# A routing search of ten steps instead of eleven, and a token order made over eight periods instead of three

## The reference, cut to what matters

```python
x = L0_attn_x                      # 16 batches x 512 tokens x 256
xn = _layernorm(x, axis=-1)
x = x + attention(xn, Wq, Wk, Wv, Wo, qn_w, kn_w) + ffn(xn, centroids, ln_g, ln_b, w1, b1, w2, b2)

# attention: 16 heads of 16; q and k normalized per head (rms), softmax, Wo
# ffn: a mixture of 8 experts with balanced assignment
def balanced_assignment(scores):   # T = 8192 tokens, E = 8, C = T // E = 1024
    taken = jnp.zeros((T,), dtype=bool)
    for e in range(E):
        s = jnp.where(taken, -jnp.inf, scores[:, e])
        _, idx = jax.lax.top_k(s, C)
        parts.append(idx)
        taken = taken.at[idx].set(True)
    return jnp.concatenate(parts)
# routed = feat[order]; out = routed + w2(gelu(w1(layer_norm(routed)))); put back by the inverse order
```

## Time and profile before

| | us |
|---|---|
| median of three runs | 1078.44 |
| lowest and highest | 1077.86, 1079.5 |
| the profiled execution, its own time | 1079.18 |
| its span in the profile | 1077.4 |
| TensorE busy in it | 1038.7 (96%) |
| VectorE busy | 802.4 (74%) |
| ScalarE busy | 744.2 (69%) |
| GpSimd busy | 714.3 (66%) |

### The profile page before, as it was taken

The page is one execution under the profiler, slowest core; times in us unless marked ns, Lnnn a source line. Parts: engine busy times, 40 slices in busy tenths (PEclk is TensorE's granted clock), DMA queues, the critical chain, the costliest instruction groups (busy, mean ns, idle before and its releaser), DMA issues.

```text
span 1077.4 us, 20796 instructions
## 1 busy us (share of the span) xinstructions
PE 1038.7 (96%) x7222; PEld 673.6 (63%) x7222; DVE 802.4 (74%) x1893; ACT 744.2 (69%) x966; POOL 714.3 (66%) x753
## 2 busy tenths in 40 slices
PE   4899999999999999999999998999999999999997
PEld 3445555454544454545454443589888999988897
DVE  8899896777777768777767678786768767777861
ACT  3588888888888888888888886763555555355550
POOL 5677878676767767677687656646665676766434
PEclk9899999999999999999999999999999999999999
DMA  4544744443443543534534455133534334453313
GB/s 154 187 158 141 241 163 144 145 163 125 160 165 109 188 146 109 206 119 139 176 128 154 151 176 173 67 104 82 128 54 123 82 82 93 89 129 53 65 20 40
DMA packets 83531, 138.15 MB, mean 128 GB/s; under 512 B 9937, under 2 KB 35793, under 8 KB 83409
## 3 DMA queue, kind: packets, MB, share of 16 engines
q1 hardware_dynamic: 54560, 103.05, 28.1%
q0 software_dynamic: 12288, 16.79, 9.1%
q10 hardware_dynamic: 16560, 16.78, 4.7%
HBM read 86.25 MB, written 50.33 MB: 127 GB/s over the span
## 4 chain that ended last, share of the span: by engine, by line
PE 84%; DVE 5%; issue 5%; ACT 4%; ACTq 1%; POOL 1%; POOLq 0%; another core or an unknown queue 0%; DVEq 0%
PE pv L507 18%; PE W L1485 16%; PE S L1471 16%; PE S L492 14%; PE W L451 9%; PE W L462 4%; PE W L476 3%; ACT prob L708 3%; PE R L421 1%; PE R L1457 1%; PE R L432 1%; PE pv L1457 1%; ACT lg L688 1%; ACTq L702 1%; DVE xb L1029 0%
## 5 line engine op out<-in xcount | busy, mean ns | idle before, releaser
L708 ACT ACTIVATE prob<-S 128x1024 f32<-128x1024 f32 x512 | 498.4, 1022 | 103.8 <-PE S L492 102.7
L507 PE MATMUL pv<-prob,v 128*17 128x512 f32 x2048 | 248.3, 598 | 0.5 <-DVE oT L873 0.5
L492 PE MATMUL S<-stq,stk 64*128 64x512 f32 x1024 | 201.6, 458 | 9.0 <-ACT prob L708 6.3
L492 PEld LDWEIGHTS S<-stq,stk 64*128 64x128 f32 x1024 | 85.2, 185 | 139.6 <-ACT prob L708 110.5
L1747 POOL DMA_INDIRECT out<-prob,order_rows x64 | 105.7, 1652 | 48.1 <-DVE prob L1687 37.1
L507 PEld LDWEIGHTS pv<-prob,v 128*17 128x17 f32 x2048 | 46.1, 96 | 116.1 <-issue 114.6
L1210 POOL TENSOR_TENSOR sq<-raw 128x512 f32<-128x512 f32 x62 | 64.6, 1042 | 74.0 <-DVE raw L840 48.6
L1547 ACT ACTIVATE wq_act<-S,b 128x512 f32<-128x512 f32 x64 | 43.7, 685 | 94.7 <-PE S L1471 89.2
L1471 PE MATMUL S<-raw_nT,xT_w 128*128 128x512 f32 x384 | 91.1, 395 | 0.0
L1240 POOL TENSOR_TENSOR lo<-full,hi 128x512 fp32r<-128x512 f32 x62 | 80.0, 1290 | 5.0
L1471 PEld LDWEIGHTS S<-raw_nT,xT_w 128*128 128x128 f32 x384 | 71.6, 188 | 17.7 <-issue 1.7
(11 more groups left out here) (257 smaller groups left out, 2595.0 us busy)
## 6 DMA issues: line engine op xcount, KB each, us to landing
stk<-parts SPq DMA_DIRECT2D x93, 256.0 KB, 3.4
stq<-parts SPq DMA_DIRECT2D x93, 256.0 KB, 4.4
xT<-in_w SPq DMA_DIRECT2D x32, 512.0 KB
parts<-hi SPq DMA_DIRECT2D x63, 256.0 KB, 2.1
parts<-lo SPq DMA_DIRECT2D x63, 256.0 KB, 2.1
out<-ao ACTq DMA_DIRECT2D x32, 256.0 KB, 4.0
xb<-in_x ACTq DMA_DIRECT2D x13, 512.0 KB, 4.0
xb<-in_x SPq DMA_DIRECT2D x2, 512.0 KB, 5.1
```

Of the source, the lines that this page charges most:

```text
L492: ins = e.matmul(S[n % 2][:, h, :], stack["k"][u][64 * h:64 * h + 64, p, c * P:(c + 1) * P], stack["q"][u][64 * h:64 * h + 64, p, :], star ...
L507: ins = e.matmul(pv[32 * j:32 * j + VW, :], v[b % 2][:, c, 8 * u + 4 * g + j, :], prob[(2 * t + j // 2) % RING][:, j % 2, :], start=(c == ...
L708: e.activation(prob[n % RING][:, :, :], S[n % 2][:, :, :], ACT.Exp).then_inc(s_exp, 1)
```

## The change

The candidates of a step may now differ in number. `HIGH_BITS` is six steps of three bits, `LOW_BITS_OF` four steps of 4, 4, 3 and 3 bits (14 in all), so `STEPS` is 10 and `ROUNDS` is 11. Steps 6 and 7 compare with 15 candidates; `ge`, `part_cnt`, `gem` and the table `cand` are made for 15. The search of the seventh expert ends in period 108, the slots are known in 110, and `ORDER` is 111.

`ordered(at)` gives one i a period, from 111 to 118; `keep_order` comes in 119. Outside lean periods TensorE's part stands behind the projections (and ahead of the routing matmul), in lean periods where it was. Two smaller edits: of the table of token numbers only the first column was ever used, and only it is loaded now; the copies of the index table for the order are made in period 103 instead of 110.

```diff
-BITS = 3
-CAND = 2 ** BITS - 1
-LOW_BITS = 14
-HIGH_STEPS = (32 - LOW_BITS) // BITS
-LOW_STEPS = -(-LOW_BITS // BITS)
-STEPS = HIGH_STEPS + LOW_STEPS
+HIGH_BITS = [3, 3, 3, 3, 3, 3]
+LOW_BITS_OF = [4, 4, 3, 3]
+BITS_OF = HIGH_BITS + LOW_BITS_OF
+LOW_BITS = sum(LOW_BITS_OF)
+HIGH_STEPS = len(HIGH_BITS)
+STEPS = len(BITS_OF)
+CANDS = [2 ** n - 1 for n in BITS_OF]
+CAND = max(CANDS)
...
 def ordered(at):
 
-    return {ORDER: (0, 1), ORDER + 1: (2, 3, 4), ORDER + 2: (5, 6, 7)}.get(at, ())
+    return (at - ORDER,) if 0 <= at - ORDER < PERIODS else ()
...
-    tokens = sb("tokens", [P, NT])
+    tokens = sb("tokens", [P, 1])
...
-            e.matmul(R[:, 0:CAND], ones_h[:, :], part_cnt[:, :], start=True, stop=True).then_inc(r_cnt, 1)
+            e.matmul(R[:, 0:CANDS[i]], ones_h[:, :], part_cnt[:, 0:CANDS[i]], start=True, stop=True).then_inc(r_cnt, 1)
...
                     score_x(e, scored(at - 3))
-                for i in ordered(at - 1):
-                    order_tensor(e, i)
+                if lean:
+                    for i in ordered(at - 1):
+                        order_tensor(e, i)
...
                     project_o(e, b - 1, kk - 4)
+                if not lean:
+                    for i in ordered(at - 1):
+                        order_tensor(e, i)
...
-        e.scalar_tensor_tensor(ge[:, :, :], key.unsqueeze(1).broadcast_to([P, CAND, NT]), best[:, 0:1],
-                               cand[:, i, :].unsqueeze(2).broadcast_to([P, CAND, NT]), ALU.subtract, ALU.is_ge).then_inc(r_ge, 1)
+        m = CANDS[i]
+        e.scalar_tensor_tensor(ge[:, 0:m, :], key.unsqueeze(1).broadcast_to([P, m, NT]), best[:, 0:1],
+                               cand[:, i, 0:m].unsqueeze(2).broadcast_to([P, m, NT]), ALU.subtract, ALU.is_ge).then_inc(r_ge, 1)
         e.wait_ge(r_ge, n + 1)
-        e.tensor_reduce(part_cnt[:, :], ge[:, :, :], AX.X, ALU.add).then_inc(r_pc, 1)
+        e.tensor_reduce(part_cnt[:, 0:m], ge[:, 0:m, :], AX.X, ALU.add).then_inc(r_pc, 1)
...
-                if at == ORDER + 3:
+                if at == ORDER + PERIODS:
                     keep_order(e)
```

More of the change, by code:

```diff
@@ L38 @@
 TAKEN = -2.0 ** 21 * UNIT
-STEP = [UNIT * 2.0 ** (BITS * i) for i in reversed(range(HIGH_STEPS))] + [2.0 ** (BITS * i) for i in reversed(range(LOW_STEPS))]
+STEP = [UNIT * 2.0 ** sum(HIGH_BITS[i + 1:]) for i in range(HIGH_STEPS)]
+STEP += [2.0 ** sum(LOW_BITS_OF[i + 1:]) for i in range(STEPS - HIGH_STEPS)]
 PRODUCTS = ((0, 0), (0, 1), (1, 0))
@@ L947, in answer @@
         e.wait_ge(r_cnt, n + 1)
-        e.tensor_scalar(gem[:, :], R[:, 0:CAND], float(C), None, ALU.is_ge, ALU.add, accum_out=digit[:, :]).then_inc(r_dg, 1)
+        e.tensor_scalar(gem[:, 0:CANDS[i]], R[:, 0:CANDS[i]], float(C), None, ALU.is_ge, ALU.add, accum_out=digit[:, :]).then_inc(r_dg, 1)
         e.wait_ge(r_dg, n + 1)
@@ L1817 @@
         "ident": np.eye(P, dtype=np.float32),
-        "tokens": (np.arange(NT)[None, :] * P + np.arange(P)[:, None]).astype(np.float32),
+        "tokens": np.arange(P, dtype=np.float32)[:, None],
         "iota": np.broadcast_to(np.arange(P, dtype=np.float32)[None], (P, P)),
```

## The result

The changed kernel takes 1071.76 us in the median of six runs (1070.42 to 1073.37), the kernel before 1078.81 in six runs (1077.86 to 1079.5): a ratio of 0.9935, with 95% between 0.9924 and 0.9945, or 7.0 us less. The profiled execution took 1071.84 us and has a span of 1070.1; predicted were 1072.7, 1073.5 profiled and 1071.7 of span. A second series on another chip gave 1068.97 against 1075.2 us, ratio 0.9941 [0.9927, 0.9955]; one of its nine executions of the kernel before took 3366 us and is left out of that ratio.

A forecast was written before the change was run, and what follows sets the result against it. TensorE, busy 96% of the span, was taken as the bound. Order stage -8.7, six groups +3.0, counts -0.8, wide steps +0.8 give -5.7 us: median 1072.7 us, range 1070.3 to 1077.0; chance 0.62 for 1071 to 1075.

The forecast's parts named there:

- the order stage: Last batch, periods 118 to 123: 33.8 us become 25.1 with two order groups left; saves 8.7 us, ends 7.4 and 9.7.
- the counts: Search: one count matmul less for each of seven experts, 0.11 us each; saves 0.8 us, or 0 if hidden.
- the wide steps' stalls: Search: two 15-candidate steps an expert, +1.1 us of VectorE each; TensorE loses 0.8 us for all seven, ends 0 and 2.2.
- the six groups: Order groups moved into TensorE-bound periods 112 to 117: 0.5 us each, +3.0 us, ends 2.8 and 3.8.
- The clock in that stage: TensorE's clock, 0.57 of full from 651 to 655 us, would be full from 640 to 660 us; not counted separately.
- VectorE's columns: One order step a period on VectorE, 2 to 3 us beside GpSimd; counted as nothing, 1 to 2 us if uncovered.
- The place of the tight period: Search: VectorE overruns worst at expert 1 (periods 49, 50), 0.6 to 1 us late; next expert 3 (71, 72), 0 to 1.
- Rival 3: Order groups in their new place still wait for VectorE, 8 x 0.7 us or more; 1078.3 us, chance 0.05.
- Rival 1: More is hidden: last batch at 4.01 us a period, its two groups free, search never stalls; -7.7, 1070.7 us, chance 0.13.
- Rivals 2 and 4: 2: VectorE late at several places, 1075.9 us, chance 0.12; 4: all 14 wide periods stall TensorE, 1082.4 us, chance 0.08.

The follow-up runs named there:

- e1: Changed kernel with the order's steps two, three and three in periods 111 to 113, TensorE's groups in 112 to 114; 1074.54 us, ratio 0.9966.
- e8: Changed kernel with the order two periods later (columns in 113 to 120, TensorE's groups in 114 to 121), search untouched; 1071.28 us, ratio 0.9938.
- e3: Changed kernel with 15 candidates compared in all ten search steps; 1075.04 us, ratio 0.9974.
- e4: Changed kernel with the search begun in period 34 instead of 32, first split spread over 32 and 33, order two periods later; 1071.00 us, ratio 0.9935.
- e6: Changed kernel with nine search steps, five wide, begun in period 39, first split spread over 37 and 38, order unmoved; 1070.36 us, ratio 0.9929.
- e7: Kernel before with only the small token table (one column instead of 64); 1078.23 us, ratio 1.0003 to the kernel before.
- r1: The changed kernel run again, unedited, on a third chip; 1068.97 us, ratio 0.9941 to the kernel before.
- r2: The nine-step kernel of e6 run again, beside r1 on the same chip; 1066.84 us, ratio 0.9930 to the kernel before.
- e2: Changed kernel with TensorE's order group ahead of the last two heads in all periods, one step a period kept; 1071.60 us, ratio 0.9940.
- e5: Changed kernel with three of the five pieces of the first score split moved to the end of VectorE's period 31; 1071.41 us, ratio 0.9943.

## Why the prediction was right, point by point

**The whole.** Predicted -5.7 us in the trace, measured -6.24 with the start equal and -7.34 in the first pair. The median fell by 7.0 us in one series and 6.2 in the other. The mechanism was right: nearly all of the gain is the order stage. That the sum is so near is in part luck. Two of its four terms, -0.8 for the counts and +0.8 for the wide steps' stalls, were both 0 when measured, and cancelled; the stage gained 0.5 us more than forecast and the six groups cost 0.3 less, which is 0.8 us, and 0.5 us were lost in places that no term named: -6.0 us in the first pair, its start taken off.

**The order stage: right, somewhat small.** -8.7 predicted, -9.21 measured, within the ends of 7.4 and 9.7. The five other periods came out at 3.94 to 4.37 us where I took 4.1 and 0.3 for a group: 121 to 123 take 3.94 to 4.04, and 120, which has no group but stands behind the last one, 4.28. e1 gives the stage without a group: 23.96 us for the six, 3.99 a period, so my 4.1 was too much, and the two groups cost 0.6 us together, which is what I counted. From 647.55 us on ScalarE did 15 softmax instructions without a gap in 14.95 us, 4 us a period, so TensorE's 4.26 for 122 and 123 before was not the pace of a period: e1 has 3.96 and 4.03 there. It is at least in part an after-effect of the order groups, since e8, which has no stall, also takes 4.28 in the period behind its last group. Of the groups, that of 118 cost nothing (3.99 us for the period, 4.03 in e1 without one), that of 119 0.33 in its own period and 0.33 in the next.

**The clock in that stage: right.** From 640 to 660 us it is 1.00; from 651 to 655 us it was 0.57. In e1, whose waits stand in longer periods with projections between them, it stayed 1.00 as well, from 600 to 625 us. Waits of the same length did not bring the low level there, so it is shown that it went with the edit, but not that the waits alone had made it.

**Six groups: right, somewhat too large.** I took 0.5 us each, from half of a group of 16, with 2.8 us as the lower end. The six cost 2.67 us, 0.42 to 0.49 each, a little under that end. The row next to it, 0.56 from start to next heads, is further off: the time from a start to what follows overstates what the group adds to a period, since the gap ahead of the heads shrinks with it in.

**The counts: the term that was not there.** I took 0.11 us each from the same kind of reading and -0.8 us for seven. Periods with a count matmul take 4.80 us, and so do those without (e8, 112 and 113). The prediction had named this case (0 if it is hidden) and not taken it. The net of both terms, 2.2 us predicted, was 2.67.

**VectorE's columns: right.** One step beside GpSimd's work, then one without:

```profile
607.03 1.11 DVE L1038 TENSOR_TENSOR xT<-xb,slot_p 128x1024 bf16<-128x1024 bf16 x1
...
612.21 0.68 DVE L1038 TENSOR_TENSOR xT<-xb,slot_p 128x1024 bf16<-128x1024 bf16 x1
```

Its eight instances take 0.68 to 1.77 us, and the four instructions of a step 2.1 us here from 611.36 us on, 4.0 in the longest, which begins at 617.20 with all four held up (0.96, 1.77, 0.70, 0.83 us). No matmul of TensorE is late for it.

**The wide steps: cost right, consequence not there.** The two lines, count and min/median/max ns:

```profile
L948 DVE SCALAR_TENSOR_TENSOR ge<-R,cand x70: 689/690/1223, 214.7 to 579.2; 128x448 bf16<-128x448 f32 x56, 128x960 bf16<-128x960 f32 x14
```

```profile
L951 DVE TENSOR_REDUCE part_cnt<-ge x70: 622/622/1157, 215.5 to 580.0; 128x7 bf16<-128x448 bf16 x56, 128x15 bf16<-128x960 bf16 x14
```

0.533 and 0.535 us more for 512 more elements, together 1.07 us, predicted 1.1. The comparison comes out at 1.22 us, I had 1.30. The Trainium skill (VectorE: DVE Perf Modes, The TRN2 errata — SBUF-src ops pay a fixed extra latency per instruction) has a fixed cost and one element per cycle at 0.96 GHz; by it 512 elements are 0.533 us, an estimate, and the trace agrees with that slope. But of the 0.8 us that I took for stalls none came. The worst place was period 49, and it is there as I had put it together:

```profile
295.05 0.17 DVE L956 TENSOR_SCALAR_CACHE_REDUCE gem<-R 128x7 f32<-128x7 f32 x1 [1.21 <-PE R L542]
...
295.92 1.22 DVE L948 SCALAR_TENSOR_TENSOR ge<-R,cand 128x960 bf16<-128x960 f32 x1
...
300.60 0.69 DVE L922 TENSOR_SCALAR scores<-xb 128x64 f32<-128x64 int32 x1
301.21 0.18 DVE L923 TENSOR_SCALAR xb<-xb 128x64 int32<-128x64 int32 x1
...
302.98 1.16 DVE L951 TENSOR_REDUCE part_cnt<-ge 128x15 bf16<-128x960 bf16 x1
...
304.67 0.68 DVE L880 STREAM_TRANSPOSE oT<-pv 128x512 f32<-128x512 f32 x1
```

From the answer at 295.05 to the next one, right behind the last split, at 301.32 us are 6.27 us, where I had 6.5 to 7.5. The second step ends at 304.14, its count matmul runs at 304.71; the transpose of pv ends at 305.35, and the weighing that needs it starts at 305.50 us: 0.15 us ahead. So it was close, and what decided was small: 0.07 us less for each comparison, the split near its cheap end (0.87 us for both, between 0.55 and 1.5), and instructions that overlap by some 0.1 us each, so that a sum of lengths is too much. A sum of differences between starts would have been the better one.

**The place of the tight period.** I named 49 and 71 and had period 32 as the example only. The single stall of the search is still that one (0.43 and 0.46 us after, as in the earlier trace rows), in all kernels with the first split unspread but e3, which has more; e4 and e6 win 1.1 us by it.

**The rivals.** Rival 3, that the stall only moves, was wrong for the change and half right for e1, which moves without spreading: it kept the waits. Rival 1, more is hidden, had the pace of the lean periods and the search without a stall right; its two groups at nothing cost 0.6 us, and its 0.8 for the counts was not there. Rivals 2 and 4 had a VectorE that is late; e3 shows that even 70 wide steps cost 3 to 4.5 us.

**What was not foreseen.** The 1.3 us at the start; they were in no term, and are an accident of the pair of traces; the one edit that touches the start, the table, is worth nothing (e7). What stays open is the 0.14 to 0.36 us lost in 124 to 127, and some 0.16 of the 0.34 us between 17 and 112, of which no row shows a wait. The low stretch of the clock that the kernel before has once from 700 to 735 us (mean 0.95) is also in the traces of after, e1, e7 and e8, and not in r1, r2 and e2 to e6 (1.00). The part from period 128 to the end is 391.3 to 391.5 us with it and 389.9 in e2 to e6: 1.5 us that have nothing to do with the edits. So medians that lie within 1.5 us of each other rank no two kernels here, unless the traces say where the difference arose. On the third chip, without it, the part takes 387.7 us; why it is shorter there is open.

## What to carry to other kernels

A producer's work that a program-ordered engine waits for costs most where that engine's own periods are short; move it to where the periods are long, and give each step a whole period between making and use: here the move alone was worth a third (traces) to a half (medians), the spreading the rest. What a matmul group costs on the engine that bounds the period is read from whole periods with and without it; from its start to the start of what follows, a group of 0.42 us looked like 0.56 and a count matmul of 0 like 0.11. Before work is moved ahead in a program, look at what stands between the two places: between those of e5 stood nothing. And whether more work fits on an engine off the path is asked of the period in which several of its rare jobs meet, not of its mean load: 91% busy cost 3.3 us in the median and 4.5 in the trace, nearly all of it in five periods.

## What the runs showed of the hardware that I had not expected

TensorE's granted clock from 30 to 45 us was 0.77, 0.89 or 1.00 in executions of programs that do the same there, worth up to 1.3 us; a comparison of two traces that does not take off such a stretch mistakes it for the change. And instructions of 128x64 elements, 0.13 and 0.15 us at their shortest, took 1.16 and 1.23 us on VectorE when they began just behind a GpSimd instruction of 1.3 us (e5); a comparison of 128x1024 took 1.77 us against 0.68 (after). A small instruction is held up by about as much as a large one.
